# Moving edge-record scatters out of the dense layers and the router into the expert tiles, behind each tile's result scatter and row fetch

## The chip, the cores and the metric

The kernel runs on one core of a Trainium2 chip. The metric is the device time of one execution in microseconds; for the kernel before, three executions were timed and the median counts. One further execution was taken by the hardware profiler, and all rows below come from that one.

## What is computed

Four blocks run one after the other over 3125 nodes of 256 features, each on the layer-normalised rows and added back to them. Cut to what matters (`ln` is the layer norm):

```python
x = x + gin(ln(x), edges)                 # segment_sum(x[src], dst), then four dense layers with batch norm and elu
x = x + moe(ln(x))                        # router: softmax, top 2 of 8 experts, gated sum of silu(x w1) * (x w3) @ w2
x = x + gat(ln(x), edges)                 # exp(leaky_relu(el[src] + er[dst])), segment_sum of w * x[dst] by src, 4 heads
x = x + ffn(ln(x))                        # the 63 highest of every row block through a gelu layer, scattered back
```

There are 50000 edges, sorted by `dst`. The first block can gather with the edges as they are; the third needs them grouped by `src`, in blocks of 125 nodes. So each edge's record (its `src` within the block and its `dst`, two integers of 4 bytes) is written to its place in a table in HBM, `rec_d`, at some time between the first block and the third.

## The kernel before

The program is a row of stages, each one block of code on five engines, with a barrier of all engines between two stages: gather and segment sum; dense layers; router and experts; tables for the third block; its edge loop; the last block.

**Records.** The edges lie in 392 columns of 128. `record(pool, t)` (L589) issues one indirect DMA on GpSimd (POOL, L590): 128 records of 8 bytes each go from `rec` to the rows of `rec_d` that column `t` of `posd` names. Nothing in the stage with the dense layers or in the experts reads `rec_d`; it is loaded in the stage behind the experts. The 392 columns are issued in three places, and constants say how many in each: 264 in the dense layers from the moment at which `posd` is known (L622), 16 in the router (L1017), and two in each of the 56 expert tiles (L1045). At the end of the expert stage POOL waits until all records (`s_sc`, L1051) and all results have landed.

**Experts.** After the router each of 56 tiles holds 128 (node, expert) pairs. Over tile t run:

- POOL, `fetch(t)` (L1025): gathers the tile's 128 rows from HBM into one of four buffers `xs`. It may be issued for tile t+4 once TensorE has turned tile t (`s_xsT`).
- PE, `turn` (L1389): transposes the rows; then the up products (L1400), the turned hidden rows (L1411) and the down products (L1421). In the code of iteration t TensorE first turns tile t+2, then does the up products of t+1 between those of t, then the down products of t. Iterations 0 to 7 are written out, 8 to 51 are a loop of four, the rest is written out again.
- ACT, `result` (L1111): scales the down product into one of two buffers `yv`; it needs the result scatter of tile t-2 to have landed.
- POOL, `give(t)` (L1034): adds the 128 result rows into `x2_d` in HBM (a scatter that accumulates). It waits for `yv` of tile t and for the scatter of tile t-1 to have landed (`s_yst`).

POOL issues everything in program order, so a DMA that waits holds all that stand behind it. In each turn of the loop at L1044 POOL issues the tile's two records, then `fetch(t + 4)`, then `give(t)`.

Of the kernel before, what the change touches and what calls it, by code (L numbers as in the profile page):

```python
# [58 lines left out]
T2 = (K2 * N + X * 127) // 128  # L59
# [51 lines left out]
def program(nc, a, out):  # L111
    with ExitStack() as ctx:
# [12 lines left out]
        def at(name, offset, shape, dt=F32):  # L125
            return nc.alloc_sbuf_tensor_at(name, shape, dt, offset=BASE + offset)

        def dram(name, shape, dt=F32):
            return nc.dram_tensor(name, shape, dt, kind="Internal").ap()
# [107 lines left out]
        with ExitStack() as p1:  # L237
# [11 lines left out]
            @block.sync  # L249
            def _(sp):  # L250
                sp.dma_start(dst_i[:, :], a["dst"]).then_inc(s_edges, 16)
                sp.dma_start(src_i[:, :], a["src"]).then_inc(s_edges, 16)
                for c in range(5):
                    for lo, hi in SPLIT:
                        sp.dma_start(x[lo:hi, CH * c:CH * (c + 1), :],
                                     a["x"].rearrange("(b p) d -> p b d", p=PB)[lo:hi, CH * c:CH * (c + 1), :]).then_inc(s_x[c], 16)
                    if c == 0:
                        sp.dma_start(eps1[:, :], a["L0_gnn_eps"].partition_broadcast(128)).then_inc(s_eps, 16)
                for c in range(5):
                    sp.wait_ge(s_xn, CH * (c + 1))  # L260
                    for lo, hi in SPLIT:
                        sp.dma_start(xn_d.rearrange("(b p) d -> p b d", p=PB)[lo:hi, CH * c:CH * (c + 1), :],
                                     x[lo:hi, CH * c:CH * (c + 1), :]).then_inc(s_xnst, 16)
                    if c < 4:
                        piece(sp, c)
                for n in range(4, len(pieces)):
                    piece(sp, n)
                sp.dma_start(W1[:, :, :], a["L0_gnn_W1"].rearrange("(k p) n -> p k n", p=128)).then_inc(s_w1, 16)
                sp.wait_ge(s_rec0, 1)
                sp.dma_start(rec_d, rec0[:, :]).then_inc(s_recst, 16)  # L270

                for l in range(3):
                    for j, name in enumerate(("b", "g", "beta")):
                        sp.dma_start(vec[:, j, 4 * VAT[l]:4 * VAT[l + 1]], a[f"L0_gnn_{name}{l + 1}"]).then_inc(s_vec, 16)
# [238 lines left out]
        behind = at("behind", 101 * KB, [T3 // HT, HT, NB])  # L513
        blk_i = at("blk_i", 101 * KB + 512, [T3 // HT, HT], I32)
        posd = at("posd", 1 * KB + 3136, [128, T1], I32)
        EDGES_EARLY = 264
        EDGES_ROUTER = 16
        PER_TILE = (T1 - EDGES_EARLY - EDGES_ROUTER) // T2
        assert EDGES_EARLY + EDGES_ROUTER + PER_TILE * T2 == T1
        blk_d = dram("blk_d", (1, T3), I32)  # L520
# [57 lines left out]
        with ExitStack() as p2:  # L578
# [10 lines left out]
            def record(pool, t):  # L589
                pool.indirect_dma_start(  # L590
                    out=rec_d.rearrange("p (t r) -> (p t) r", r=2),
                    out_offset=bass.IndirectOffsetOnAxis(ap=posd[:, t:t + 1], axis=0),
                    in_=rec[:, t, :], in_offset=None).then_inc(s_sc[t % 2], 16)
# [22 lines left out]
            def _(pool):  # L616
# [4 lines left out]
                pool.wait_ge(s_pos, 1)  # L621
                for t in range(EDGES_EARLY):  # L622
                    record(pool, t)
# [289 lines left out]
        XB = 4  # L913
# [48 lines left out]
        with ExitStack() as p3:  # L962
# [33 lines left out]
            @block.gpsimd  # L996
            def _(pool):
                ch = Chain(pool, s_c3[0])
                nc.gpsimd.memset(ones3[:, :], 1.0)
                ch.step(nc.gpsimd.memset(later3[:, :], 1.0))  # L1000
                ch.step(nc.gpsimd.affine_select(out=later3[:, :], in_=later3[:, :], compare_op=ALU.is_gt, fill=0.0,
                                                base=0, pattern=[[1, PB]], channel_multiplier=-1))
                ch.step(nc.gpsimd.iota(person[:, :], pattern=[[0, 1]], base=0, channel_multiplier=1,
                                       allow_small_or_imprecise_dtypes=True))
                ch.step(nc.gpsimd.iota(spare[:, :], pattern=[[0, 1]], base=N + 1, channel_multiplier=1,
                                       allow_small_or_imprecise_dtypes=True))
                pool.sem_inc(s_k3, 1)
                nd = xn2_d.rearrange("(b p) d -> p b d", p=PB)
                rd = x2_d[0:N, :].rearrange("(b p) d -> p b d", p=PB)
                for c in range(5):  # L1010
                    cs = slice(5 * c, 5 * c + 5)
                    pool.wait_ge(s_n3, 5 * c + 5)
                    for lo, hi in SPLIT:
                        pool.dma_start(nd[lo:hi, cs, :], xn2[lo:hi, cs, :]).then_inc(s_xn2st, 16)
                for lo, hi in SPLIT:
                    pool.dma_start(rd[lo:hi, :, :], x2[lo:hi, :, :]).then_inc(s_x2st, 16)
                for t in range(EDGES_EARLY, EDGES_EARLY + EDGES_ROUTER):  # L1017
                    record(pool, t)
                nc.clear_and_free_semaphores(done)


                def fetch(t):
                    if t >= XB:
                        pool.wait_ge(s_xsT, t - XB + 1)
                    pool.indirect_dma_start(  # L1025
                        out=xs[:, t % XB, :], out_offset=None, in_=xn2_d,
                        in_offset=bass.IndirectOffsetOnAxis(ap=from_i[:, t:t + 1], axis=0)).then_inc(s_xs[t % XB], 16)

                def give(t):
                    i = t % 2  # L1030
                    pool.wait_ge(s_yv, 1 + t + 1)
                    if t:
                        pool.wait_ge(s_yst[1 - i], 16 * ((t - 1) // 2 + 1))
                    pool.indirect_dma_start(  # L1034
                        out=x2_d, out_offset=bass.IndirectOffsetOnAxis(ap=to_i[:, t:t + 1], axis=0),
                        in_=yv[:, i, :], in_offset=None, compute_op=ALU.add).then_inc(s_yst[i], 16)

                pool.wait_ge(s_xn2st, 160)
                pool.wait_ge(s_where, 1)
                for t in range(XB):  # L1040
                    fetch(t)
                pool.wait_ge(s_x2st, 32)
                pool.wait_ge(s_zst, 16)
                for t in range(T2):  # L1044
                    for j in range(PER_TILE):  # L1045
                        record(pool, EDGES_EARLY + EDGES_ROUTER + t * PER_TILE + j)
                    if t + XB < T2:
                        fetch(t + XB)
                    give(t)
                for i in range(2):  # L1050
                    pool.wait_ge(s_sc[i], 16 * (T1 // 2))  # L1051
                for i in range(2):
                    pool.wait_ge(s_yst[i], 16 * (T2 // 2))
# [1291 lines left out]
```

## Time and profile before

| | us |
|---|---|
| median of three executions | 2200.62 (2200.25 to 2207.63) |
| the profiled execution | 2197.58 |
| its span, first to last instruction | 2195.9 |
| dense layers, records issued in them (264) | from 586.05 to 942.98 |
| router and experts | from 946.55 to 1438.43 |
| expert tiles, first to last result scatter | from 1049.35 to 1430.14 |

Busy shares of the whole span (PE 83%, DVE 63%, POOL 61%, ACT 31%) are averages over stages with different limits, so they say little here. What counts for this change is what POOL does between two result scatters of the expert loop, what it waits for there, and what it is doing when the two stages end.

### The profile page before, as it was taken

The numbers are of one execution on the slowest core, as the hardware profiler recorded it, in microseconds if no ns is written. First come the engines' busy times: TensorE is split into PE (matmuls) and PEld (weight loads), VectorE is DVE, ScalarE is ACT, GpSimd is POOL, SyncE is SP. The second block draws the span as 40 slices with busy tenths as digits, with TensorE's granted clock in tenths as the row PEclk, the third lists the DMA queues.
The fourth block names the chain that finished last, engine by engine and source line by source line (L and its number), as shares of the span: only waits on it lengthen the run. The fifth ranks groups of instructions, "written<-read, shape, count | busy, mean of one in ns | idle before, by whom it ended". The sixth has DMA issues, their size and how long they took to land. (4 is left out here: it accounts for less than half of the span.)

```text
span 2195.9 us, 36674 instructions
## 1 busy us (share of the span) xinstructions
PE 1830.5 (83%) x9636; PEld 1305.5 (59%) x9637; DVE 1374.3 (63%) x3193; ACT 670.3 (31%) x1334; POOL 1347.9 (61%) x1358
## 2 busy tenths in 40 slices
PE   2898999888899799663899999947878887885888
PEld 2776777666344345562666666645656665664666
DVE  7766654444755686778733333346777777777766
ACT  4000000000455665635633333332111111111874
POOL 3777777776277777742566666527777777774000
PEclk8555555555999799855999999977898889887999
DMA  8333333333000300272122222252111111113002
GB/s 247 98 105 103 105 105 105 105 104 90 0 1 1 60 1 1 83 282 88 30 39 39 39 39 39 30 123 40 28 28 28 28 29 28 29 28 13 1 1 59
DMA packets 95358, 132.05 MB, mean 60 GB/s; under 512 B 34959, under 2 KB 66334, under 8 KB 95293
## 3 DMA queue, kind: packets, MB, share of 16 engines
q0 software_dynamic: 57312, 87.64, 18.3%
q1 hardware_dynamic: 37981, 43.65, 6.9%
q8 instruction: 27, 0.44, 0.1%
q14 instruction: 38, 0.31, 0.0%
HBM read 109.24 MB, written 21.96 MB: 60 GB/s over the span
## 5 line engine op out<-in xcount | busy, mean ns | idle before, releaser
L590 POOL DMA_INDIRECT rec_d<-rec,posd x392 | 396.0, 1010 | 166.9 <-issue 125.6
L491 PE MATMUL psA<-oh,G 128*128 128x128 f32 x1568 | 444.2, 448 | 61.2 <-DMA G<-xn_d,gat_i 29.8
L1670 POOL DMA_INDIRECT g<-tab_d,recs x416 | 395.1, 950 | 160.3 <-issue 126.5
L306 POOL DMA_INDIRECT G<-xn_d,gat_i x392 | 376.6, 961 | 146.1 <-issue 137.4
L491 PEld LDWEIGHTS psA<-oh,G 128*128 128x128 f32 x1568 | 351.6, 313 | 153.7 <-issue 98.2
L1819 PE MATMUL psS<-vv,oh 128*125 128x260 f32 x832 | 288.7, 494 | 90.8 <-DVE acc L1751 90.8
L835 PE MATMUL psZ<-z,W 128*128 (+1 forms) x1344 | 264.4, 360 | 24.0 <-DVE z L734 24.0
L1819 PEld LDWEIGHTS psS<-vv,oh 128*125 128x125 f32 x832 | 160.9, 225 | 188.8 <-DVE acc L1751 161.3
L441 DVE TENSOR_TENSOR accT<-accT,psA 128x256 f32 x392 | 164.9, 421 | 166.4 <-PE psA L491 140.5
L636 ACT ACTIVATE z<-psZ,vec 128x500 f32 (+2 forms) x112 | 70.7, 633 | 638.1 <-PE psZ L828 527.9
L835 PEld LDWEIGHTS psZ<-z,W 128*128 128x128 f16 x1344 | 124.7, 99 | 163.7 <-issue 37.0
L1400 PE MATMUL psH<-we,xh 128*128 x1344 | 214.6, 310 | 2.2 <-issue 2.0
L1751 DVE TENSOR_TENSOR acc<-acc,psS 125x260 f32 x416 | 176.5, 424 | 33.7 <-PE psS L1819 1.8
L1679 ACT ACTIVATE ohT<-psOT 125x512 f32<-125x512 f32 x104 | 62.1, 597 | 352.5 <-PE psOT L1803 352.5
L1400 PEld LDWEIGHTS psH<-we,xh 128*128 128x128 f16 x1344 | 131.3, 98 | 60.2 <-issue 7.2
L1034 POOL DMA_INDIRECT x_d<-yv,to_i x56 | 91.7, 1638 | 100.3 <-ACT yv L1111 99.8
L1740 DVE TENSOR_TENSOR vv<-g,psP 128x1040 f32<-128x1040 f32 x104 | 127.8, 1229 | 25.8 <-PE psS L1819 17.0
L1421 PE MATMUL psY<-we,hh 128*128 (+1 forms) x1008 | 127.5, 275 | 11.0 <-DVE hh L1295 11.0
L1288 DVE SCALAR_TENSOR_TENSOR hv<-psH,sl 128x384 f32<-128x384 f32 x112 | 57.4, 512 | 118.7 <-ACT sl L1099 118.7
L1811 PEld LDWEIGHTS psE<-el,ohT 125*128 125x128 f32 x832 | 119.8, 209 | 17.4 <-issue 7.6
L1421 PEld LDWEIGHTS psY<-we,hh 128*128 128x128 f16 (+1 forms) x1008 | 86.4, 97 | 45.8 <-issue 25.0
L1811 PE MATMUL psE<-el,ohT 125*128 x832 | 107.9, 253 | 6.2 <-DVE psP L1727 5.3
(323 smaller groups left out, 2433.3 us busy)
## 6 DMA issues: line engine op xcount, KB each, us to landing
raw<-in_L_ffn_w SPq DMA_DIRECT2D x16, 682.0 KB, 8.6
g<-tab_d,recs POOLq DMA_INDIRECT x416, 2.5
G<-xn_d,gat_i POOLq DMA_INDIRECT x392, 2.7
rec_d<-rec,posd POOLq DMA_INDIRECT x392
raw<-in_L_ffn_w SPq DMA_DIRECT2D x16, 384.0 KB, 10.1
wst<-in_L_gnn_W SPq DMA_DIRECT2D x9, 512.0 KB, 6.8
x<-in_x SPq DMA_DIRECT2D x5, 560.0 KB
xn_d<-x SPq DMA_DIRECT2D x5, 560.0 KB
```

Of the source, the lines that this page charges most:

```text
L306: pool.indirect_dma_start(out=G[:, i, :], out_offset=None, in_=xn_d, in_offset=bass.IndirectOffsetOnAxis(ap=gat_i[:, t:t + 1], axis=0)).th ...
L441: nc.vector.tensor_tensor(accT[:, :, bass.ds(at_[i], WIN)], accT[:, :, bass.ds(at_[i], WIN)], psA[i // 2][:, i % 2, :, :], ALU.add).then_i ...
L491: last = nc.tensor.matmul(psA[i // 2][:, i % 2, h, :], G[:, i, 128 * h:128 * (h + 1)], oh[:, i, :], start=True, stop=True)
L590: pool.indirect_dma_start(out=rec_d.rearrange("p (t r) -> (p t) r", r=2), out_offset=bass.IndirectOffsetOnAxis(ap=posd[:, t:t + 1], axis=0 ...
L835: last = nc.tensor.matmul(psZ[m % 4][:, 0:w], W[l][:, sw, k, ms], halves(l, k, c * CW, w)[sh], start=(n == 0), stop=(n == len(terms) - 1))
L1400: last = nc.tensor.matmul(psH[2 * w3 + q][:, 0:HC[q]], xh[:, i, sx, 128 * k:128 * (k + 1)], weights(e, 2 * w3 + k, sw, q * HQ, HC[q]), sta ...
L1421: last = nc.tensor.matmul(psY[:, :], hh[0:KP[m], i, sh, 128 * m:128 * (m + 1)], weights(e, 4 + n, sw, (m - 3 * n) * D, D)[0:KP[m], :], sta ...
L1670: pool.indirect_dma_start(out=g3[:, n % BODY, j, :], out_offset=None, in_=tab_d, in_offset=bass.IndirectOffsetOnAxis(ap=recs[:, t, 1:2], a ...
L1740: nc.vector.tensor_tensor(vv[:, s % 2, :, :].rearrange("p j (h f) -> p j h f", h=NH), g3[:, s, :, NH:RW].unsqueeze(2).to_broadcast([128, H ...
L1751: nc.vector.tensor_tensor(b, b, psS[j][:, :], ALU.add).then_inc(s_ac, 1)
L1811: last = nc.tensor.matmul(psE[:, j, :], ohT[:, s % 2, 128 * j:128 * (j + 1)], el[:, bass.ds(at_[j] * NH, NH)], start=True, stop=True)
L1819: last = nc.tensor.matmul(psS[j][:, :], oh3[:, s, j, :], vv[:, s % 2, j, :], start=True, stop=True)
```

## The change

```diff
-        EDGES_EARLY = 264
-        EDGES_ROUTER = 16
+        EDGES_EARLY = 224
+        EDGES_ROUTER = 0
         PER_TILE = (T1 - EDGES_EARLY - EDGES_ROUTER) // T2
...
                 for t in range(T2):
+                    give(t)
+                    if t + XB < T2:
+                        fetch(t + XB)
                     for j in range(PER_TILE):
                         record(pool, EDGES_EARLY + EDGES_ROUTER + t * PER_TILE + j)
-                    if t + XB < T2:
-                        fetch(t + XB)
-                    give(t)
```

With T1 = 392 and T2 = 56, PER_TILE goes from 2 to 3: the dense layers issue 224 records in place of 264, the router none in place of 16, the tiles 168 in place of 112. In a tile, the result scatter and the fetch now come ahead of the records. Only POOL's order changes; the other engines have the same instructions.

On POOL in the dense layers (`rec_d<-rec` is a column of records, `zero` and `ones` the first instructions of this stage and of the router), before:

```order
222 L618 MEMSET zero 128x256
223 L590 DMA rec_d<-rec,posd 53248x2 x264
224 L578 UNCONDITIONAL_BRANCH
225 L996 UNCONDITIONAL_BRANCH
226 L999 MEMSET ones_5030 128x125
```

and after:

```order
222 L618 MEMSET zero 128x256
223 L590 DMA rec_d<-rec,posd 53248x2 x224
224 L578 UNCONDITIONAL_BRANCH
225 L996 UNCONDITIONAL_BRANCH
226 L999 MEMSET ones_4990 128x125
```

40 columns fewer stand ahead of the branch that ends the stage.

On POOL from the router to the first tile (`xs<-xn_d` is a fetch, `x_d<-yv` a result scatter), before:

```order
244 L590 DMA rec_d<-rec,posd 53248x2 x16
245 L1019 ISA x4
246 L1025 DMA xs<-xn_d,from_i 128x256 x4
247 L590 DMA rec_d<-rec,posd 53248x2 x2
248 L1025 DMA xs<-xn_d,from_i 128x256
249 L1034 DMA x_d<-yv,to_i 3253x256
```

and after:

```order
244 L1019 ISA x4
245 L1025 DMA xs<-xn_d,from_i 128x256 x4
246 L1034 DMA x_d<-yv,to_i 3253x256
247 L1025 DMA xs<-xn_d,from_i 128x256
248 L590 DMA rec_d<-rec,posd 53248x2 x3
249 L1034 DMA x_d<-yv,to_i 3253x256
```

Between two result scatters stood two records and a fetch; now a fetch and three records stand there, the fetch directly behind the first scatter, where it is that of tile t+4 and not of t+5.

On POOL at the end of the experts (`row` is the first instruction of the next stage), before:

```order
409 L590 DMA rec_d<-rec,posd 53248x2 x2
410 L1034 DMA x_d<-yv,to_i 3253x256
411 L962 UNCONDITIONAL_BRANCH
412 L1567 UNCONDITIONAL_BRANCH
413 L1569 MEMSET row 125x25
```

and after:

```order
408 L1034 DMA x_d<-yv,to_i 3253x256
409 L590 DMA rec_d<-rec,posd 53248x2 x3
410 L962 UNCONDITIONAL_BRANCH
411 L1567 UNCONDITIONAL_BRANCH
412 L1569 MEMSET row 125x25
```

The last DMA of the stage was a result scatter; now three records stand behind it.

## Rows read from the trace of the kernel before

**Rows 1.** Stretches: us, PE, PEld, DVE, ACT, POOL busy (x), clock, DMA share, GB/s.

```profile
820.00:880.00 60.00, 59.55 (x353) 30.11 (x350) 39.34 (x84) 33.68 (x58) 46.28 (x46) 1.00 0.02 1
1083.00:1403.00 320.00, 310.23 (x2345) 221.00 (x2343) 112.07 (x236) 116.01 (x281) 213.03 (x188) 1.00 0.25 39
```

**Rows 2.** POOL by line, 1083 to 1403: busy us, mean ns, idle before.

```profile
L590 POOL DMA_INDIRECT rec_d<-rec,posd x94 | 90.9, 967 | 28.7 <-issue 28.7
L1034 POOL DMA_INDIRECT x_d<-yv,to_i x47 | 76.1, 1619 | 65.7 <-ACT yv L1111 65.7
L1025 POOL DMA_INDIRECT xs<-xn_d,from_i x47 | 46.2, 984 | 14.3 <-issue 14.3
```

**Rows 3.** POOL's timeline, tiles 50 and 51: start, duration, operation, idle before.

```profile
1396.54 1.61 POOL L1034 DMA_INDIRECT x_d<-yv,to_i  x1 [1.22 <-ACT yv L1111]
1398.45 0.98 POOL L590 DMA_INDIRECT rec_d<-rec,posd  x1 [0.31 <-issue]
1399.74 0.96 POOL L590 DMA_INDIRECT rec_d<-rec,posd  x1 [0.30 <-issue]
1401.00 0.99 POOL L1025 DMA_INDIRECT xs<-xn_d,from_i  x1 [0.30 <-issue]
1403.03 1.61 POOL L1034 DMA_INDIRECT x_d<-yv,to_i  x1 [1.05 <-ACT yv L1111]
```

**Rows 4.** PE's timeline: the turns that open two iterations.

```profile
1388.93 0.44 PE L1389 MATMUL psTx<-ident,xs 128*128 128x128 f32 x2
1395.51 0.44 PE L1389 MATMUL psTx<-ident,xs 128*128 128x128 f32 x2
```

**Rows 5.** The tile xs: from the start of a fetch's issue to its landing.

```profile
DMA to landing us min/median/max: 2.7/2.8/6.6
```

**Rows 6.** POOL's timeline, tiles 0, 2 and 4.

```profile
1049.35 1.64 POOL L1034 DMA_INDIRECT x_d<-yv,to_i  x1 [17.32 <-ACT yv L1111]
...
1069.64 1.36 POOL L590 DMA_INDIRECT rec_d<-rec,posd  x1 [0.30 <-issue]
...
1082.80 2.01 POOL L1034 DMA_INDIRECT x_d<-yv,to_i  x1 [2.71 <-ACT yv L1111]
```

**Rows 7.** Timelines of POOL and ACT at the end of the experts.

```profile
1425.53 1.59 POOL L1034 DMA_INDIRECT x_d<-yv,to_i  x1 [2.29 <-ACT yv L1111]
...
1428.69 0.96 POOL L590 DMA_INDIRECT rec_d<-rec,posd  x1 [0.30 <-issue]
1430.14 1.58 POOL L1034 DMA_INDIRECT x_d<-yv,to_i  x1 [0.48 <-issue]
1438.43 0.14 POOL L1569 MEMSET row<- 125x25 f32 x1 [6.71 <-POOLq L962]
...
1428.96 0.47 ACT L1111 ACTIVATE yv<-psY,weight 128x256 f32<-128x256 f32 x1 [2.83 <-PE psY L1421]
```

**Rows 8.** Timelines of POOL and DVE where two stages end.

```profile
942.01 0.97 POOL L590 DMA_INDIRECT rec_d<-rec,posd  x1 [0.30 <-issue]
946.55 0.20 POOL L999 MEMSET ones<- 128x125 f32 x1 [3.58 <-POOLq L578]
...
943.24 0.42 DVE L747 SCALAR_TENSOR_TENSOR x<-psO,x 125x256 f32<-125x256 f32 x1 [0.62 <-PE psO L852]
...
543.08 0.56 DVE L461 COPY pos<-psT 128x392 f32<-128x392 f32 x1
...
544.46 0.31 POOL L618 MEMSET zero<- 128x256 f32 x1 [6.38 <-POOLq L237]
```

**Rows 9.** DVE by line, 890 to 943; a record beside it; an operation of router and experts.

```profile
L729 DVE TENSOR_SCALAR z<-yb 128x500 f32 x20 | 7.4, 414 | 0.0
...
899.62 1.19 POOL L590 DMA_INDIRECT rec_d<-rec,posd  x1 [0.30 <-issue]
...
L1173 DVE SCALAR_TENSOR_TENSOR we<-raw,we x48: 853/870/959, 976.5 to 1082.4; 128x682 f16<-128x682 f32 x32, 128x768 f16<-128x768 f32 x16
```

**Rows 10.** POOL's timeline, the first fetch behind the router.

```profile
1021.88 1.00 POOL L1025 DMA_INDIRECT xs<-xn_d,from_i  x1 [24.99 <-DVEq L1278]
```

## The prediction

> **What bounds the kernel now.** I read the stages first, then POOL in each of the three places that the change touches, then the ends of two stages. In the steady part of the expert loop TensorE is the bound: 310.2 of 320 us busy, at a granted clock of 1.00, that is 2.4 GHz, all through [rows 1]. POOL is busy for 213 us of the same stretch, so an average leaves it a third of the time. But per tile the room is small, and that is the view to read: POOL waits 65.7 us in 47 tiles for the result of ACT before a result scatter [rows 2], 1.40 us a tile, and a DMA that waits for nothing still has 0.30 us ahead of it [rows 3]. So 1.10 us a tile is free. In the dense layers and the router POOL's records are beside other work: the router's are over 25 us before POOL gets its first fetch to issue, since that waits for DVE [rows 10]. The DMA engines are no part of the question: with records alone running they are 2% busy [rows 1].
>
> **The change part by part.**
>
> *One more record per tile.* A record costs POOL 0.97 us and 0.30 us of gap, 1.27 in all [rows 2, 3]. That is more than the 1.10 us that are free. POOL's round now is 213.2 us busy, 43.0 us of gaps and 47 times 0.30, over 47 tiles: 5.75 us [rows 2]. With a third record it is 7.02. The tiles run from the scatter of tile 4, at 1082.80, to that of tile 51, at 1403.03, in 320.2 us, 6.81 a tile [rows 3, 6]. 47 rounds of 7.02 are 330.0 us: POOL comes out of the loop 9.8 us later. No wait has to appear anywhere for this; POOL simply never idles.
>
> Who waits for that? Not ACT, which has two tiles of room, but TensorE, at the turn of tile t+4, whose fetch now stands directly behind the result scatter of tile t. The fetch starts 1.91 us after that scatter [rows 3] and lands 2.8 us later [rows 5], at 4.7. TensorE needs 6.58 us from turn to turn [rows 4], and the next scatter of POOL comes 1.03 us after the turn behind it (1395.51 to 1396.54) [rows 3, 4]. So two tiles need at least 4.7 + 6.58 + 1.03 = 12.3 us, and POOL's two rounds are 14.0: the fetch's new place is not the bound, and POOL may lag by up to 1.7 us before TensorE feels it. **Term 1: 9.8 - 1.7 = 8.1 us.** In tiles 1 to 3 POOL's DMAs are slower (a record of 1.36 us, a scatter of 2.01), but the first four tiles also take 8.4 us each (1049.35 to 1082.80) [rows 6]; at worst 0.6 us more.
>
> *The last two tiles.* No fetch is left from tile 52 on, so POOL catches up, but the end is tight. The last two result scatters start 4.61 us apart, and the second could hardly start earlier: ACT's result is done at 1429.43 and POOL's record at 1429.65 [rows 7]. With three records between them POOL needs 1.9 + 3 x 1.27 = 5.7. **Term 2: 1.1 us.**
>
> *Three records behind the last scatter.* Now the next stage opens 8.29 us after the last scatter's start (1430.14 to 1438.43). That of tile 55 waits for that of tile 54 to land, so 54 landed within 4.61 us; then some 3.7 us are left in which POOL leaves the stage [rows 7]. After the change the last record's issue ends 1.9 + 2 x 1.27 + 0.96 = 5.4 us after that scatter's start. When it lands, no row shows: a fetch lands 1.8 us after its issue ends (2.8 - 0.98), a result scatter at most 3.0 (4.61 - 1.59). I take 2.2, nearer to the fetch, because a record carries no data to speak of. 5.4 + 2.2 + 3.7 = 11.3 in place of 8.3. The bounds are 0.7 (if leaving starts with the last issue, as at the end of the dense layers, 5.4 + 3.6) and 3.8. **Term 3: 3.0 us.** The Trainium skill (DMA: Bandwidth & Descriptors, Anatomy of one DMA) puts some 2.0 us of fixed cost on a small DMA from GpSimd, most of it the receipt of the write, longest for HBM; with that the term would be an estimated 2.8. No run here shows a record's landing.
>
> *40 records fewer in the dense layers.* POOL is done some 60 us earlier. DVE's last operation ends at 943.66, POOL's last record at 942.98, and the router opens at 946.55, 2.9 us after DVE and 3.6 after POOL [rows 8]. At the end of the gather stage, where POOL had been done for long, the next stage opened 0.82 us after DVE's last operation [rows 8]. So it is probably POOL that the barrier waits for: it needs 3.6 us to leave the stage, much as the 3.7 us at the end of the experts. Without it the router opens at 943.66 + 0.82. **Term 4: -2.1 us**, with 0 as the other end if another engine is late there.
>
> *16 records fewer in the router*: nothing, by the 25 us of waiting above. *The first tile* now gets its scatter ahead of the fetch of tile 4, but it lands 4.7 us behind that scatter, and TensorE turns tile 4 only at the next tile's result, 8.4 us later; nothing.
>
> **The sum**: 8.1 + 1.1 + 3.0 - 2.1 = +10.1 us. The profiled execution, 2197.58, becomes 2207.7. The median of the runs shown is 3.0 us above it, so the median becomes 2200.62 + 10.1 = **2210.7**. By the bounds of the terms alone it is 7.3 (8.1 + 1.1 + 0.7 - 2.6) to 13.6 (8.7 + 1.1 + 3.8): 2207.9 to 2214.2.
>
> **The rivals.**
>
> *The barrier gains nothing.* If the 2.9 us between DVE and the router are another engine's, term 4 is zero: +12.2, 2212.8. For it: no row names POOL as the last one, it is found by exclusion. Against it: DVE, which ends last, needed 0.82 at the other place. 20%.
>
> *The fetch behind the scatter comes late.* Now two records, 2.5 us, stand between a result scatter and the fetch behind it, and the trace cannot show how long a fetch takes directly behind one. If its rows start to move only once the scatter has landed, it lands at 4.61 + 1.8 = 6.4 us, just where two tiles take POOL's 14.0; with 1 us more two tiles take 15.0, 0.5 us a tile above POOL's round, and 47 tiles bring 23 us and the lost 1.7 on top: some 2235. The point from which it decides is a landing 4.5 us after the fetch's start. The first fetch did take 6.6 [rows 5], but beside a load of expert weights. 8%.
>
> *Not slower: the dense layers get quicker.* Their last 53 us are a chain of DVE and ACT, and records there take 1.19 us in place of 0.97 when DVE works [rows 9]. If DVE lost time to records in the same way, taking 40 of them away would give it back: 0.25 us for each record would bring 10.1 us and make the change free, 2200.6; 0.4 would make it 2194.6. The Trainium skill (SBUF — State Buffer, Who interferes with whom) says that DVE and GpSimd share a pair of ports by an exclusive lock and that the loser waits in full, which would allow this. The rows speak against it: the 20 operations of L729 have one duration, 414 ns, beside records of either length, and L1173 has a median of 870 ns and a maximum of 959 for both of its widths over the router, where records run beside it, and the first tiles, where for long they do not [rows 9]. It is POOL that waits. 5%.
>
> That the change does not do what it says can be left out: the order shows 224 and three behind each scatter.
>
> **How the numbers follow.** The forecast, +10.1, has 65%, the barrier 20%, the late fetch 8%, the quicker dense layers 5%, and 2% are left for what I don't see. The range reaches a little over the bounds of the terms, 2205.5 to 2216, and leaves out the late fetch and the quicker dense layers. A measurement of this kernel can tell about 0.5% from no change, 11 us: slower by over that is at 2211.6. A fifth of the forecast's spread lies above it (0.13), most of the barrier's (0.17) and all of the late fetch (0.08): 0.38. Faster by over 0.5% needs the dense layers far quicker: 0.03. The rest, 0.59, is within 0.5%.
>
> **What would show it.** In the loop: POOL without a wait before the result scatters, rounds of 7.0 us, three records of 0.97, and TensorE waiting at its turns for the fetch's DMA, 0.2 us a tile. A wait longer than that, with POOL idle for ACT, is the late fetch. At the end: the last scatter 5.7 us behind the one before it, and the next stage some 11 us behind that. At the router: an opening 0.8 us after DVE's last operation (2.9 is the rival). DVE's 414 ns should stay. I am wrong if POOL still idles in the loop, or if a record takes less there than 0.97 us.

## The result, and the profile after

The changed kernel takes 2211.6 us (median of 5 runs, 2209.0 to 2214.5); the kernel before, run beside it, 2203.95 (2200.3 to 2207.6). The medians differ by 7.65 us; the ratio of all runs is 1.0045 with a 95% interval of [1.0031, 1.0059], some 10 us slower. Forecast were 2210.7 and a range of 2205.5 to 2216, from a median before of 2200.62; beside the changed kernel it was 3.3 us higher. The profiled execution has a span of 2209.5 us in place of 2195.9. The rows of both traces split these 13.6 us by the prediction's steps:

| step | forecast | measured |
|---|---|---|
| the router opens (946.55, now 944.00) | -2.1 | -2.55 |
| from there to the scatter of tile 4 | 0 (at most 0.6) | +0.27 |
| scatter of tile 4 to that of tile 51 (320.23, now 329.70) | +9.8 | +9.47 |
| tile 51 to 52, where TensorE is the bound again (9.60, now 8.79) | -1.7 | -0.81 |
| tile 52 to 54 (12.90, now 12.90) | 0 | 0.00 |
| tile 54 to 55 (4.61, now 5.70) | +1.1 | +1.09 |
| scatter of tile 55 to the next stage (8.29, now 12.66) | +3.0 | +4.37 |
| from there to the end (757.47, now 759.23) | 0 | +1.76 |
| sum | +10.1 | +13.60 |

POOL in the changed kernel by line, 1090 to 1410 us of the span (busy us, mean ns, idle before); it answers to [rows 2]:

```profile
L590 POOL DMA_INDIRECT rec_d<-rec,posd x138 | 132.9, 963 | 42.1 <-issue 42.1
L1034 POOL DMA_INDIRECT x_d<-yv,to_i x45 | 72.1, 1603 | 13.9 <-issue 13.4 <-ACT yv L1111 0.4
L1025 POOL DMA_INDIRECT xs<-xn_d,from_i x46 | 45.8, 996 | 14.0 <-issue 14.0
```

The wait for ACT, 65.7 us in 47 tiles before, is 0.4 us in 45. Every DMA now stands 0.30 us behind the one ahead of it. POOL's timeline of one tile (start, duration, operation, idle before; it answers to [rows 3]):

```profile
1396.21 1.61 POOL L1034 DMA_INDIRECT x_d<-yv,to_i  x1 [0.30 <-issue]
1398.12 0.99 POOL L1025 DMA_INDIRECT xs<-xn_d,from_i  x1 [0.30 <-issue]
1399.42 0.97 POOL L590 DMA_INDIRECT rec_d<-rec,posd  x1 [0.30 <-issue]
1400.69 0.96 POOL L590 DMA_INDIRECT rec_d<-rec,posd  x1 [0.30 <-issue]
1401.96 0.95 POOL L590 DMA_INDIRECT rec_d<-rec,posd  x1 [0.30 <-issue]
1403.21 1.60 POOL L1034 DMA_INDIRECT x_d<-yv,to_i  x1 [0.30 <-issue]
```

That is a round of 7.00 us, where [rows 2] gave 5.75 us and 1.40 of waiting. TensorE's waits of the changed kernel, 1090 to 1400 (us in total, times, longest), and two of its turns in the timeline, which answer to [rows 4]:

```profile
PE psTx L1389 <- DMA xs<-xn_d,from_i: 12.5, 20, 1.8
...
1394.94 0.43 PE L1389 MATMUL psTx<-ident,xs 128*128 128x128 f32 x2 [0.41 <-DMA xs<-xn_d,from_i]
...
1402.33 0.43 PE L1389 MATMUL psTx<-ident,xs 128*128 128x128 f32 x2 [0.62 <-DMA xs<-xn_d,from_i]
```

Before, no turn of this stretch waited for a fetch. The landing of `xs` in the last fetches, between 1365 and 1412, from the start of the issue (minimum, median, maximum), first in the kernel before, then in the changed one, where the 2.8 is a fetch ahead of the last five; [rows 5] had 2.7/2.8/6.6 for the whole loop:

```profile
DMA to landing us min/median/max: 3.5/3.7/3.9
```

```profile
DMA to landing us min/median/max: 2.8/3.6/4.1
```

At the opening of the router, DVE's last operation of the dense layers and POOL's first of the router, changed kernel ([rows 8]):

```profile
943.29 0.42 DVE L747 SCALAR_TENSOR_TENSOR x<-psO,x 125x256 f32<-125x256 f32 x1 [0.62 <-PE psO L852]
...
944.00 0.20 POOL L999 MEMSET ones<- 128x125 f32 x1 [59.91 <-POOLq L578]
```

POOL had been done for 60 us, and the router opens 0.29 us behind DVE (943.71) in place of 2.89. The end of the expert stage, POOL's timeline ([rows 7]):

```profile
1431.91 1.59 POOL L1034 DMA_INDIRECT x_d<-yv,to_i  x1 [1.02 <-ACT yv L1111]
...
1437.61 1.59 POOL L1034 DMA_INDIRECT x_d<-yv,to_i  x1 [0.30 <-issue]
...
1442.05 0.96 POOL L590 DMA_INDIRECT rec_d<-rec,posd  x1 [0.30 <-issue]
1450.27 0.14 POOL L1569 MEMSET row<- 125x25 f32 x1 [7.26 <-POOLq L962]
```

The last issue ends 5.40 us behind the start of the last scatter, as forecast; then come 7.26 us, where 2.2 + 3.7 = 5.9 were forecast.

The views by line also show what POOL does when it leaves a stage: its sequencer has one instruction DRAIN there, its last before the barrier (minimum, median and maximum in ns, first and last start in us; what it waits for, no row says). At the end of the experts, before and after:

```profile
L962 POOLq DRAIN  x1: 3732/3732/3732, 1434.4 to 1434.4; - x1
...
L962 POOLq DRAIN  x1: 5284/5284/5284, 1444.7 to 1444.7; - x1
```

It ends 0.25 us before the next stage opens in both, after the DRAIN of every other engine. So the longer leaving is a longer DRAIN, 5.28 us in place of 3.73.

### The profile page after: what moved, and what is told of

It reads as the page before. It is cut to its first block and busy times, and to the rows that moved or that the text cites. A ratio compares the mean times of both kernels' runs of the same rounds, so it can differ in the third digit from the quotient of the medians.

```text
span 2209.5 us, 36674 instructions
## 1 busy us (share of the span) xinstructions
PE 1819.4 (82%) x9636; PEld 1290.0 (58%) x9637; DVE 1375.1 (62%) x3193; ACT 672.1 (30%) x1334; POOL 1345.3 (61%) x1358
## 5 line engine op out<-in xcount | busy, mean ns | idle before, releaser
L491 PE MATMUL psA<-oh,G 128*128 128x128 f32 x1568 | 432.8, 439 | 72.7 <-DMA G<-xn_d,gat_i 40.6
L491 PEld LDWEIGHTS psA<-oh,G 128*128 128x128 f32 x1568 | 342.1, 305 | 163.3 <-issue 98.2
L1819 PEld LDWEIGHTS psS<-vv,oh 128*125 128x125 f32 x832 | 155.9, 220 | 195.3 <-DVE acc L1751 167.7
```

The source lines that it names most:

```text
L491: last = nc.tensor.matmul(psA[i // 2][:, i % 2, h, :], G[:, i, 128 * h:128 * (h + 1)], oh[:, i, :], start=True, stop=True)
L1819: last = nc.tensor.matmul(psS[j][:, :], oh3[:, s, j, :], vv[:, s % 2, j, :], start=True, stop=True)
```

## The experiments

The kernel before ran beside all of them. Experiments 5, 7 to 10 and 12 were run once, for their traces, and no ratio is given for them. In "early / router / per tile" it is 264 / 16 / 2 and the changed kernel 224 / 0 / 3. Unless said otherwise the diffs are against the kernel before.

**1. The order alone.** 264 / 16 / 2 as before, but records behind the scatter and the fetch.

```diff
-                    for j in range(PER_TILE):
-                        record(pool, EDGES_EARLY + EDGES_ROUTER + t * PER_TILE + j)
+                    give(t)
                     if t + XB < T2:
                         fetch(t + XB)
-                    give(t)
+                    for j in range(PER_TILE):
+                        record(pool, EDGES_EARLY + EDGES_ROUTER + t * PER_TILE + j)
```

> The changed order in a tile (result scatter, fetch, records) with the old counts: 264 records in the dense layers, 16 in the router, two per tile. My theory (POOL's round is the bound in the changed kernel, the order costs only at the end): a round of 5.75 us stays under the tiles' 6.81, so the loop keeps 320.2 us from the scatter of tile 4 to that of tile 51 and the router opens at 946.6; behind the last scatter stand two records, so the next stage opens some 11.4 us after that scatter's start in place of 8.3: +3.1 us in all. Rival (the fetch directly behind the scatter comes late): TensorE waits for fetches in most turns and the loop is longer by 10 us or more.

Measured: 1.0004 [0.9993, 1.0015], no difference that can be measured. Tiles 4 to 51 take 320.9 us (320.2 before), so the fetch behind the scatter is not late: that rival falls. The end is 9.91 us in place of 8.29, +1.6 where +3.1 was expected, with two records behind the last scatter. So 5.78 us pass behind the last issue, less than in the changed kernel: the first sign that the 7.26 there are not simply a landing and a fixed rest.

**2. The counts alone.** 224 / 0 / 3 in the old order.

```diff
-        EDGES_EARLY = 264
-        EDGES_ROUTER = 16
+        EDGES_EARLY = 224
+        EDGES_ROUTER = 0
```

> The changed counts (224, none in the router, three per tile) in the old order: records, fetch, result scatter. My theory: POOL's round is 7.02 us again and the scatters of tiles 4 and 51 stand 330 us apart, but a fetch is now issued one tile earlier, so POOL may lag by some 4.9 us before TensorE feels it, in place of 1.7. TensorE is then 4.9 us late at the end of the loop (8.9 in the changed kernel), the last scatter 1.1 more, nothing stands behind it (8.3 us to the next stage), and the router opens 2.5 us earlier: +3.5 to +4 us against the kernel before, some 8 us under the changed kernel. Rival (the number of records alone sets the cost, not their place): about the +11.8 us of the changed kernel at the opening of the next stage, less only the 4.4 us at the end.

Measured: 1.0022 [1.0013, 1.0031], half of the loss. Tiles 4 to 51 take 329.62 us, as in the changed kernel: the round of 7.0 us comes from the third record, whatever the order. But tile 52 is only 5.8 us later than before, counted from the router's opening, and 8.9 in the changed kernel. POOL's timeline of one tile in the old order shows why:

```profile
1401.36 0.99 POOL L1025 DMA_INDIRECT xs<-xn_d,from_i  x1 [0.30 <-issue]
1402.65 1.61 POOL L1034 DMA_INDIRECT x_d<-yv,to_i  x1 [0.30 <-issue]
```

Here the fetch starts 1.29 us ahead of the scatter, in the changed kernel 1.91 behind it. That is 3.20 us later for the same lag of POOL, and TensorE comes out of the loop 3.1 us later. So the new order costs 3.1 us at the loop's end, once POOL is the bound, and nothing in the loop. The end is 10.10 us here, with nothing behind the last scatter, where 8.29 were expected; experiments 8 to 10 are about that.

**3. The gain at the router alone.** 248 / 32 / 2, the old order.

```diff
-        EDGES_EARLY = 264
-        EDGES_ROUTER = 16
+        EDGES_EARLY = 248
+        EDGES_ROUTER = 32
```

> The kernel before with 16 records moved from the dense layers to the router (248 and 32), tiles as before. My theory (POOL leaves the dense layers last, 3.6 us after its last record): the router opens 0.3 to 0.8 us after DVE's last operation in place of 2.9, 2.5 us earlier; 32 records in the router end some 5 us before POOL's first fetch, so all that follows moves by -2.5 us. Rival (what the dense layers gain comes from fewer records in all, or the router's records cost): the router opens at 946.6 as before, or the first fetch comes as late as before.

Measured: 0.9992 [0.9982, 1.0001]. The router opens 0.29 us behind DVE, as in the changed kernel: POOL is the engine that the barrier waits for, and the rival of term 4 falls. But the first fetch comes 79.5 us behind the opening, 75.3 before, which takes the gain back. Records of the router and DVE's operations beside them, timelines of POOL and DVE in this kernel:

```profile
1000.19 0.95 POOL L590 DMA_INDIRECT rec_d<-rec,posd  x1 [0.31 <-issue]
...
1006.40 2.29 POOL L590 DMA_INDIRECT rec_d<-rec,posd  x1 [0.30 <-issue]
...
1021.84 1.37 POOL L590 DMA_INDIRECT rec_d<-rec,posd  x1 [0.30 <-issue]
1025.29 1.67 POOL L1025 DMA_INDIRECT xs<-xn_d,from_i  x1 [2.07 <-issue]
...
1005.95 1.91 DVE L1260 TENSOR_TENSOR valt<-oht,vals 125x1680 f16<-125x1680 f16 x1
...
1020.41 0.21 DVE L1277 TENSOR_TENSOR to_i<-found 128x56 int32<-128x56 f32 x1
```

DVE has the indices ready at 1020.62, but POOL's 32 records end at 1023.21, since those beside DVE's L1253 to L1260 take up to 2.29 us, and 2.07 more pass before the fetch. So records in the router are free only as long as they end before that.

**4. The last tile's records ahead** of its scatter's turn, in the changed kernel: its three records are issued before tile 0, so that nothing stands behind the last scatter (diff against the changed kernel).

```diff
+                for j in range(PER_TILE):
+                    record(pool, T1 - PER_TILE + j)
                 for t in range(T2):
                     give(t)
                     if t + XB < T2:
                         fetch(t + XB)
+                    if t == T2 - 1:
+                        continue
```

> The changed kernel with the three records of the last tile issued ahead of the first result scatter, where POOL waits for over 20 us; nothing stands behind the last scatter. My theory (a record lands late, and POOL leaves the stage only after it): the next stage opens 8.3 us after the last scatter's start in place of 12.7, so -4.4 us against the changed kernel, with the same loop (328.6 us from tile 4 to tile 51). Rival (the wait at the end is POOL's own leaving after 392 records, wherever they stand): 12.7 us stay.

Measured: 1.0036 [1.0023, 1.0049]; its interval overlaps the changed kernel's. The end is 10.15 us, 2.5 shorter than the 12.66 and not back at 8.29, like experiment 2: with three records per tile 8.5 us pass behind a last issue that is a scatter, with two 6.7.

**5. When a record has landed.** In the kernel before, POOL waits at the end of the dense layers for its 264 records to land and then writes a mark.

```diff
                 for t in range(EDGES_EARLY):
                     record(pool, t)
+                for i in range(2):
+                    pool.wait_ge(s_sc[i], 16 * (EDGES_EARLY // 2))
+                nc.gpsimd.memset(mark[:, :], 0.0)
```

> The kernel before, with POOL waiting behind its last record of the dense layers until all 264 have landed, and a small memset behind that wait as a mark in the trace. Theory A (a record lands some 3.6 us after its issue ends, and POOL needs a further 3.6 us to leave a stage): the mark stands at 946.6 and the router opens at 950.2, 3.6 us later than before. Theory B (the 3.6 us in which POOL leaves are its last record's landing): the mark stands at 946.3 and the router opens within 0.8 us of it. Theory C (a record lands 2.2 us after its issue ends): the mark stands at 945.2.

POOL's timeline there:

```profile
943.77 0.97 POOL L591 DMA_INDIRECT rec_d<-rec,posd  x1 [0.30 <-issue]
946.00 0.10 POOL L627 MEMSET mark<- 128x1 f32 x1 [1.25 <-DMA rec_d<-rec,posd]
949.67 0.20 POOL L1003 MEMSET ones<- 128x125 f32 x1 [3.57 <-POOLq L579]
```

The record has landed 1.25 us behind the end of its issue, 2.2 behind its start. The wait doesn't shorten what comes after: 3.57 us, the 3.58 of [rows 8]. So with 264 records POOL needs 3.6 us to leave this stage from its last instruction on, whether its DMAs have landed or not. These 3.6 us are again the DRAIN's end and 0.25 us, and they are no fixed price. POOL's DRAIN at the end of the gather stage and of the dense layers in the kernel before, and at the end of the dense layers in the changed kernel:

```profile
L237 POOLq DRAIN  x1: 11031/11031/11031, 533.2 to 533.2; - x1
L578 POOLq DRAIN  x1: 19822/19822/19822, 926.5 to 926.5; - x1
...
L578 POOLq DRAIN  x1: 25362/25362/25362, 868.3 to 868.3; - x1
```

The DRAIN begins while issues are still under way, so its end counts. Before, in the dense layers, it ends at 946.30, 3.3 us behind the last record, and DVE's ends at 943.7: POOL holds the barrier. In the changed kernel, with 224 records, it ends at 893.69, 9.6 us behind the last record (884.10), which costs nothing there. In the other runs it ends 4.6 us behind the last of 168 records, 2.2 behind 248 and 3.0 behind 260. What it follows, no run tells.

**6. Last records first, at two per tile.** 248 / 32 / 2, the old order, the last tile's two records ahead of tile 0.

```diff
+                for j in range(PER_TILE):
+                    record(pool, T1 - PER_TILE + j)
                 for t in range(T2):
-                    for j in range(PER_TILE):
+                    for j in range(PER_TILE if t < T2 - 1 else 0):
```

> The kernel before with 248 records in the dense layers and 32 in the router, two per tile ahead of the fetch as before, but the two records of the last tile ahead of the first, where POOL waits. My theory: -2.5 us at the router, and the last result scatter starts when its tile is ready and its forerunner has landed, up to 0.4 us earlier: -2.5 to -2.9 us against the kernel before. Rival (the barrier's gain is given back in the router or the tiles): no change.

Measured: 0.9996 [0.9985, 1.0008], no difference. Behind tile 51 hardly anything is shorter than in experiment 3 (tile 54 to 55 4.57 us for 4.59, the end 8.21 for 8.44): moving the last records ahead brings next to nothing, and the rival of the expectation holds; and the router loses as in experiment 3.

**7. Four per tile**, 168 / 0 / 4, the new order: if POOL is the bound of the loop, each record more costs its 1.27 us in full (diff against the changed kernel).

```diff
-        EDGES_EARLY = 224
+        EDGES_EARLY = 168
         EDGES_ROUTER = 0
```

> The changed order with 168 records in the dense layers, none in the router and four per tile. My theory (POOL's round is the bound): a round is 7.02 + 1.27 = 8.29 us, so the scatters of tiles 4 and 51 stand 390 us apart in place of 320 (before) and 329 (changed): TensorE is some 65 us late. Rival (TensorE's waits come from the fetch's place, and records hide behind TensorE's own waits): clearly less than +60 us from the changed kernel to this one.

POOL by line, 1095 to 1475:

```profile
L590 POOL DMA_INDIRECT rec_d<-rec,posd x184 | 176.8, 961 | 56.1 <-issue 56.1
L1034 POOL DMA_INDIRECT x_d<-yv,to_i x46 | 73.7, 1603 | 14.0 <-issue 14.0
L1025 POOL DMA_INDIRECT xs<-xn_d,from_i x46 | 45.8, 996 | 14.0 <-issue 14.0
```

Tiles 4 to 51 take 388.8 us (390 expected), 8.27 a tile, 1.26 more than with three. The third record cost 9.5 us because 1.1 of its 1.27 us a tile were still free; the fourth costs 59.1. The one run took 2282 us.

**8 to 10. What the end of the expert stage is made of.** Three marks behind the last tile: after the last issue, after the waits for all records, after the waits for all result scatters. In the changed kernel (8), in the kernel before (9), and in 224 / 0 / 3 of the old order (10); each diff is against the kernel named, and it is the same in all three.

```diff
+                nc.gpsimd.memset(marks[:, 0:1], 0.0)
                 for i in range(2):
                     pool.wait_ge(s_sc[i], 16 * (T1 // 2))
+                nc.gpsimd.memset(marks[:, 1:2], 0.0)
                 for i in range(2):
                     pool.wait_ge(s_yst[i], 16 * (T2 // 2))
+                nc.gpsimd.memset(marks[:, 2:3], 0.0)
```

> The changed kernel with three marks (memsets of one word on POOL) at the end of the expert stage: behind the last issue, behind the waits for all records to have landed, behind the waits for all result scatters to have landed. It splits the 7.26 us between the last record's issue and the next stage. Theory A (the last record lands late, leaving costs the 3.6 us of the dense layers): the second mark some 3.7 us behind the first, the third at once behind it, the next stage 3.6 us behind the third. Theory B (a record lands 1.3 us after its issue, as in the dense layers, and leaving costs more here): the second mark 1.3 us behind the first, the third at once, the next stage some 6 us behind it. Theory C (the last result scatter, started 12.7 us before the next stage, lands last, since the records are queued behind it): the third mark is the late one, 2 us or more behind the second. The prediction itself had 2.2 and 3.7.

> The same three marks in the kernel before, where the last result scatter is the last issue (6.71 us to the next stage). Theory A and C: the second mark at once behind the first (the records have landed), the third some 3.0 us behind (the landing of the scatter), the next stage 3.6 us behind the third. Theory B: the scatter lands sooner, the next stage 5 us or more behind the third mark.

> The same three marks in the kernel with 224 early records and three per tile ahead of the fetch and the scatter (8.51 us from the last issue, a scatter, to the next stage, where before has 6.71 with the same last instruction). If the landing makes the 1.8 us, the third mark stands 4.9 us behind the first and the next stage 3.6 us behind the third; if leaving does, the third mark stands 3.0 us behind the first and the next stage some 5.5 us behind it.

POOL's timelines from the last issue to the next stage; first the changed kernel with marks:

```profile
1447.31 0.96 POOL L590 DMA_INDIRECT rec_d<-rec,posd  x1 [0.30 <-issue]
1448.27 0.11 POOL L1051 MEMSET marks<- 128x1 f32 x1
1449.83 0.10 POOL L1054 MEMSET marks<- 128x1 f32 x1 [1.44 <-DMA rec_d<-rec,posd]
1449.91 0.10 POOL L1057 MEMSET marks<- 128x1 f32 x1
1455.55 0.14 POOL L1573 MEMSET row<- 125x25 f32 x1 [5.54 <-POOLq L963]
```

The kernel before with marks:

```profile
1433.35 1.58 POOL L1035 DMA_INDIRECT x_d<-yv,to_i  x1 [0.40 <-issue]
...
1437.02 0.10 POOL L1057 MEMSET marks<- 128x1 f32 x1 [1.94 <-DMA x_d<-yv,to_i]
1441.10 0.14 POOL L1573 MEMSET row<- 125x25 f32 x1 [3.99 <-POOLq L963]
```

The third record in the old order, with marks:

```profile
1436.00 1.59 POOL L1035 DMA_INDIRECT x_d<-yv,to_i  x1 [0.30 <-issue]
...
1439.87 0.10 POOL L1057 MEMSET marks<- 128x1 f32 x1 [2.14 <-DMA x_d<-yv,to_i]
1445.55 0.14 POOL L1573 MEMSET row<- 125x25 f32 x1 [5.58 <-POOLq L963]
```

The record has landed 1.6 us behind the end of its issue, the scatter 2.1 to 2.3 behind its own; in the changed kernel the last scatter has long landed when the last record has. In experiments 8 and 10 theory B holds; in 9 the scatter lands sooner, as it said, but the leaving is 4.0 us, not the 5 or more of theory B nor the 3.6 of theory A. So the landings differ little, and what is longer is the leaving, 5.5 us with three records per tile in either order, 4.0 with two. POOL's DRAIN says the same in every trace: 5.28 to 5.45 us in the five kernels with three records per tile, 3.57 to 3.85 in the eight with two.

**11. A better split.** 260 / 20 / 2, the old order: four records fewer in the dense layers, as POOL needed 3.6 us to leave with 264, and so few in the router that they end before the slow stretch.

```diff
-        EDGES_EARLY = 264
-        EDGES_ROUTER = 16
+        EDGES_EARLY = 260
+        EDGES_ROUTER = 20
```

> 260 records in the dense layers, 20 in the router, two per tile, the old order. POOL is done with the dense layers some 4.3 us ahead of DVE in place of 0.7, and with the router's records near 1001, before the stretch where records took 1.4 to 2.3 us. By the theory that POOL alone holds the router's opening and that the loss in the router came from the 32 records: the router opens 0.3 us behind DVE, 2.6 us earlier, the first fetch 75.3 us behind the opening as before, and the whole is 2.6 us faster, ratio 0.9988. If the router's records do not matter and DVE's later chain sets the fetch on its own: the fetch 79 us behind the opening and no gain, 1.0000.

Measured: 2195.95 us (12 runs) against 2201.71, ratio 0.998 [0.997, 0.999]: 0.2% faster than the kernel before, by a little more than the noise. POOL's timeline at the opening, at the router's last record and at the first fetch:

```profile
945.04 0.20 POOL L999 MEMSET ones<- 128x125 f32 x1 [6.22 <-POOLq L578]
...
999.47 0.96 POOL L590 DMA_INDIRECT rec_d<-rec,posd  x1 [0.30 <-issue]
1020.66 1.00 POOL L1025 DMA_INDIRECT xs<-xn_d,from_i  x1 [20.23 <-DVEq L1278]
```

POOL is done 6.2 us before the router opens, which is 0.29 us behind DVE (944.75). Its DRAIN ends at 941.83, 3.0 us behind the last record and 2.9 ahead of the end of DVE's last operation; with the 9.6 us of the 224 records it would have come too late, so that four records are enough was partly luck. The router's records end at 1000.4, the last 17 without a slow one, and the fetch still waits 20 us for DVE. It comes 75.6 us behind the opening, so the gain stays; in the traces the next stage opens 2.15 us earlier than before.

**12. What the longer leaving follows.** The marks once more, with 224 / 56 / 2 in the old order: as few early records as in the changed kernel, but two per tile (diff against the kernel of experiment 9).

```diff
-        EDGES_EARLY = 264
-        EDGES_ROUTER = 16
+        EDGES_EARLY = 224
+        EDGES_ROUTER = 56
```

> The three marks once more, with 224 records in the dense layers as in the changed kernel, but 56 in the router and two per tile, in the old order. POOL left the expert stage 5.5 us behind its third mark with 224 early and three per tile, in either order, and 4.0 us behind it with 264 early and two per tile. If the leaving follows the expert stage's own code (two or three records a tile) or POOL's lack of idle time in the loop, it is 4.0 us here; if it follows the number in the dense layers, 5.5 us. For the router: 40 records more than before, at 1.27 us and up to 2.6 us each where DVE works beside them. If they were free there, the first fetch would stay 75.3 us behind the opening; by the 32-record kernel (fetch 79.5 us behind the opening) it comes some 24 times 1.27 = 30 us later than that, 110 us behind the opening, and the whole at about 2232.

POOL's timeline at its end and at the first fetch:

```profile
1471.18 0.10 POOL L1057 MEMSET marks<- 128x1 f32 x1 [2.06 <-DMA x_d<-yv,to_i]
1475.26 0.14 POOL L1573 MEMSET row<- 125x25 f32 x1 [3.99 <-POOLq L963]
...
1060.95 1.01 POOL L1026 DMA_INDIRECT xs<-xn_d,from_i  x1 [2.07 <-issue]
```

The leaving is 3.99 us again: it does not follow the number of early records but the expert stage itself, three records per tile against two. Whether that is the length of POOL's program there, the number of its DMAs or a POOL that never idles in the loop, no run tells. Experiment 7 speaks against a plain growth with any of them: with four per tile the DRAIN takes 4.47 us, between the two. And in the dense layers POOL issues without a pause in every kernel, yet its DRAIN ends 2.2 to 9.8 us behind the last record. The first fetch comes 111.1 us behind the opening (110 expected), and the one run took 2239 us (2232 expected), 35 more than before beside it: 40 records more in the router are far from free.

## Why the prediction was right, and where its steps were off

**Term 1, the loop: right in its cause, 0.8 us too small.** POOL's round of 7.0 us and its lag of 9.8 us stand as forecast (9.5 between tiles 4 and 51, 9.7 from the opening; a record takes 0.963 us there and not 0.967, 4 ns under the prediction's sign of being wrong, which makes some 0.6 us over 141 records). The step that failed is the room of 1.7 us. It took the fetch's landing as 2.8 us, the median over the whole loop in [rows 5]; but the room counts at the loop's last tiles, and there a fetch lands in 3.5 to 3.9 us in the kernel before and in 3.6 to 4.1 in the changed one. With these the two tiles need 1.9 + 3.7 (or 4.1) + 6.58 + 1.03 = 13.2 to 13.6 of POOL's 14.0 us, a room of 0.4 to 0.8; 0.8 was measured. Why the last fetches land later isn't settled. They are those of tiles 51 to 55 in every kernel (medians of 3.7 to 3.9 in experiments 1, 3, 7 and 11), at whatever time they are issued: from 1373.6 us on before, from 1445.9 in experiment 7, where those between 1365 and 1412 still land in 2.8 at the median. So it goes with the tile, and the share of the DMA engines is the same (0.25 and 0.26). The kernel reserves 56 tiles for the worst spread of 6250 pairs, and every slot without a pair gathers row 0 (L1276), so the last tiles can be such slots alone; that many reads of one row are what is slow was not tested. Experiment 2 bears the rest out: with the fetch 3.2 us earlier in POOL's round TensorE's lag is 3.1 us smaller.

**Term 2: right**, 1.09 us.

**Term 3: right in sign, 1.4 us too small, and beyond its bound of 3.8.** Its three parts were 5.4 of issue, 2.2 of landing and 3.7 of leaving. The issue is 5.40. The landing is 1.25 to 1.6, shorter than taken. The leaving is what was mis-sized, twice. The 3.7 were a remainder, 8.29 less the 4.61 us within which the scatter of tile 54 had landed; experiment 9 shows that a scatter lands 3.7 us behind its start (1433.35 to 1437.02), so 4.1 to 4.6 are left for the leaving before. And a third record per tile makes it 1.5 us longer (the DRAIN of 5.28 us for 3.73), which no row of before could show. The Trainium skill (DMA: Bandwidth & Descriptors, Anatomy of one DMA) gave some 2.0 us of fixed cost, an estimated 2.8 for the term. The landing measured here is 2.2 to 2.5 us from the start of the issue, close to that; but the estimate had counted the 2.0 from the end of the issue, and the term hung on the leaving.

**Term 4: right.** In experiments 3 and 11 the router opens the same 2.6 us nearer to DVE's last operation, from fewer early records alone. Experiment 5 shows that those 3.6 us are POOL's leaving, not a record's landing, and a row of before could have named POOL: its DRAIN ends 2.6 us behind DVE's. The router opens 0.29 us behind DVE, not the 0.82 of the gather stage, which is the -2.55 in place of -2.1. The 0.82 was misread: POOL had issued its last gather 6.4 us before the next stage opened, but its DRAIN ended only at 544.21, 0.25 before that opening, and DVE's last operation at 543.64. There too POOL was the last, and the opening said nothing of DVE. The -2.6 in the prediction's lower bound has no row; that it was met is luck.

**16 records fewer in the router: nothing, as said**; the first fetch waits for DVE 75.2 us behind the opening, before 75.3. The 25 us of waiting that stood for it are not 25 us of free issue, though: experiments 3 and 12 show records there of up to 2.29 us.

**The rivals.** The late fetch fell with experiment 1 and the barrier that gains nothing with experiment 3. The quicker dense layers didn't come: in the changed kernel DVE's last operation there ends at 943.71 us, 943.66 before, though records ran beside it for 60 us less; counted from the opening of the stage (543.75 and 544.46) that is 0.8 us more and not less. Experiment 3 shows the same where records and DVE collide hardest: DVE's L1260 takes 1.9 us with records beside it and without, and it is the record that grows. The Trainium skill (SBUF — State Buffer, Who interferes with whom) has an exclusive lock on the ports that the two share, and the loser waiting in full; the rows agree in so far as only one of the two is longer, and it is POOL each time. They do not fit that section's inference that an operation like L1260 (`tensor_tensor`) does not stall a DMA: beside it the issue of a record took up to 2.29 us.

**The sum.** Up to the opening of the stage behind the experts the traces differ by 11.8 us where 10.1 were forecast: term 1 came out 0.8 larger and term 3 1.4, and term 4 gained 0.45 more. The mechanisms hold, and together the errors come to 1.7 us; that 2211.6 lies within 1 us of the 2210.7 is luck all the same, since the median before was 3.3 us higher in these runs.

**The rest of the program** is 1.8 us longer in the trace of the changed kernel, in stages that the change doesn't touch. It is 757.4 to 762.0 us over all kernels run here, and its cause stays open. With it the traces differ by 13.6 us, where the timed runs give 6.8 to 13.

## What to carry to other kernels

An engine that is two thirds busy can have no room for one more DMA per round: count its round, gaps included, against the round of the engine that is the bound, and once it is the bound itself, the place of each DMA in its order counts as well. Before a barrier, look at which engine's DRAIN ends last, not at which computed last: moving four DMAs out of the dense layers made this program 0.2% faster, where the change, which moved 56, made it 0.45% slower. How long that DRAIN takes has to be read anew in each variant. Durations that a term rests on should be read in the very stretch in which it decides, not as a median over the loop.

## What the runs showed of the hardware

- POOL ends a stage with a DRAIN on its sequencer. Where it is the last engine, the next stage opens 0.25 us behind that DRAIN's end. In the dense layers the DRAIN ended 4.6 us behind the last issue with 168 records (experiment 7), 9.4 to 9.8 with 224, 2.2 with 248, 3.0 with 260 and 3.3 to 3.4 with 264; at the end of the gather stage it ended 6.1 us behind the last issue in every trace. At the end of the experts it took 3.6 to 3.9 us with two records per tile, 5.3 to 5.5 with three and 4.5 with four. Waiting for the landing of its DMAs first (experiment 5) doesn't shorten it.
- A record of 128 times 8 bytes lands 1.25 to 1.6 us behind the end of its issue, an accumulating scatter of 128 rows of 1 KB 2.1 to 2.3 us behind its own, and a gather of 128 rows of 1 KB lands 2.8 us behind its start in most of the loop and 3.4 to 4.5 in that of the last five tiles, over the kernels here.
- Beside DVE operations that read two tensors in SBUF (L1260, 1.9 us), the issue of a record on POOL grows from 0.96 to up to 2.29 us (experiments 3 and 12); DVE's operation doesn't grow.
